# Sorting edges by destination block: four bf16 pieces per edge instead of six, and two one-hots cut in halves

## What is computed

```
xn  = layernorm(x)
deg = segment_sum(edge_weight, src) + 1
norm = dinv[src] * edge_weight * dinv[dst]            # dinv = 1/sqrt(deg)
h7[src] += (xn @ W)[dst] * norm                       # over all edges, and a self-loop each
x = x + MLP(h7) + mix(xn)                             # mix: attention without softmax, and an MLP
x = x + top-2-of-8-experts(layernorm(x))
```

## Time and profile before

| | us |
|---|---|
| median of 3 runs | 4314.45 |
| the profiled execution's own time | 4289.22 |
| its span | 4287.5 |
| setup, to the first work of the sort | 80 |
| the sort's first lot | 80 to 105 |
| the sort, from GpSimd's first scatter | 105 to 730 |
| rows stage | 730 to 879 |
| all that follows | 879 to 4287.5 |

### The profile page before, as it was taken

One profiled execution on the slowest core, in us unless ns is written; L12 is line 12 of the kernel. 1 busy time (PEld: TensorE's weight loads), 2 busy tenths in 40 slices (PEclk: granted clock), 3 DMA queues, 4 the chain that ended last, 5 costly groups with the idle time before them and its releaser, 6 DMA issues. The chain is left out here.

```text
span 4287.5 us, 76667 instructions
## 1 busy us (share of the span) xinstructions
PE 3246.9 (76%) x20541; PEld 2549.1 (59%) x20541; DVE 2761.6 (64%) x7400; ACT 1581.4 (37%) x4972; POOL 2678.2 (62%) x2429
## 2 busy tenths in 40 slices
PE   5778785757776677776557777777777589999995
PEld 4556564634444444444436665666666479999985
DVE  7999997946556556565545555555555665555577
ACT  2877773421111111111003333333333255555542
POOL 1888886256666666666666666666666246666663
PEclk8888887568888888888779888888888789999998
DMA  4322222543333334333334444444444412222367
GB/s 159 46 28 28 26 28 44 179 121 112 111 112 111 110 110 115 109 111 110 100 92 133 130 126 131 130 130 132 132 132 129 148 44 70 71 70 71 119 223 269
DMA packets 292326, 466.67 MB, mean 109 GB/s; under 512 B 96007, under 2 KB 197900, under 8 KB 292239
## 3 DMA queue, kind: packets, MB, share of 16 engines
q0 software_dynamic: 139776, 272.98, 24.5%
q1 hardware_dynamic: 140127, 183.95, 13.0%
q10 hardware_dynamic: 12338, 8.71, 0.6%
HBM read 361.91 MB, written 104.56 MB: 109 GB/s over the span
## 5 line engine op out<-in xcount | busy, mean ns | idle before, releaser
L1712 POOL DMA_INDIRECT rows<-table,idx x1664 | 1594.8, 958 | 879.7 <-issue 502.3
L2014 DVE TENSOR_TENSOR acc<-acc,ps_seg 128x256 f32 x1664 | 696.6, 419 | 927.2 <-remote 774.0
L2179 PE MATMUL ps_seg<-rows,pick 128*128 128x256 f32 x3328 | 1000.2, 429 | 342.3 <-DVE acc L2014 254.3
L2179 PEld LDWEIGHTS ps_seg<-rows,pick 128*128 128x128 f32 x3328 | 662.7, 213 | 526.6 <-issue 433.0
L860 POOL DMA_INDIRECT records<-sort_rec,sort_addr x280 | 531.8, 1899 | 181.0 <-issue 91.1
L1856 DVE TENSOR_SCALAR pick<-iota_row,loc,ewt 128x128 f32<-128x128 f32 x1680 | 531.8, 365 | 11.2 <-DVE loc L1852 4.4
L2632 POOL DMA_INDIRECT y_rows<-arena,spot x204 | 295.9, 1450 | 206.5 <-issue 59.0
L2774 PE MATMUL ps_h<-arena,up_now 128*128 128x128 f32 x3264 | 401.1, 276 | 3.7 <-DVE up_now L2702 2.3
L2774 PEld LDWEIGHTS ps_h<-arena,up_now 128*128 128x128 f32 x3264 | 382.1, 193 | 7.3 <-issue 7.1
L2758 PE MATMUL ps_y<-down_now,arena 128*128 128x256 f32 x1632 | 385.9, 379 | 0.0
L1058 PE MATMUL ps_out<-acc 128*128 128x240 bf16 x1568 | 266.3, 350 | 121.9 <-DVE acc L979 121.8
(11 more groups left out here) (403 smaller groups left out, 5090.1 us busy)
## 6 DMA issues: line engine op xcount, KB each, us to landing
rows<-table,idx POOLq DMA_INDIRECT x1664
acc<-y_rows SPq DMA_DIRECT2D x20, 896.0 KB
x_early<-in_x SPq DMA_DIRECT2D x118, 128.0 KB
xn<-in_x SPq DMA_DIRECT2D x100, 128.0 KB
xT_dram<-xT SPq DMA_DIRECT2D x98, 128.0 KB
xn<-xT_dram SPq DMA_DIRECT2D x49, 256.0 KB
skip<-in_x SPq DMA_DIRECT2D x98, 128.0 KB
x_rows<-acc SPq DMA_DIRECT2D x49, 256.0 KB
```

What stands on the lines that cost most here:

```text
L1712: pool.indirect_dma_start(out=rows[:, t, :], out_offset=None, in_=k.table, in_offset=bass.IndirectOffsetOnAxis(idx[:, h, t:t + 1], 0)).the ...
L2014: dve.tensor_tensor(here, here, sums(u), ALU.add).then_inc(added[u], 1)
L2179: last = pe.matmul(sums(t), pick[:, h, t, :], rows[:, t, :], start=True, stop=True)
```

## The change

An edge is now cut into four pieces. Word 0 of a record is no longer a sum but two bf16 values side by side: the low half-words of `dst | 1 << 14` and of a word that holds the seven low bits of the weight (one of them flipped), and the row. Word 1 is the sum of two bf16 parts of the weight with its seven low bits cleared. The rows stage puts the low bits back. With four pieces the products have 2 x 2240 elements, the matmuls of `compact` 160 columns, and the spread pieces 112 elements. The lane one-hot and the block one-hot are each made by two instructions of 14 columns, and `compact` and `count` on TensorE wait for each half. Records are written by two instructions, a copy that casts to bf16 pairs and a reduction.

```diff
-PIECES = 6
+PIECES = 4
+ROW_AT = 16
+ROUND_BITS = 7
...
 def same_block(dve, s, buf, lot, cut):          # 14 columns: cut * CUT to (cut + 1) * CUT
...
 # setup, ScalarE: four casts in place of six
+low_half = lambda words: words.bitcast(BF16).rearrange("p (n two) -> p n two", two=2)[:, :, 0]
+act.activation(s.pieces[:, 0, :], low_half(tmp_i), ACT.Copy)
+act.activation(s.pieces[:, 1, :], low_half(src), ACT.Copy)
+act.activation(s.pieces[:, 2, :], short_ew, ACT.Copy)
+act.activation(s.pieces[:, 3, :], rest, ACT.Copy)
...
 # setup, VectorE, between the histogram one-hots
-dve.tensor_scalar(tmp_i, src, P - 1, 14, ALU.bitwise_and, ALU.logical_shift_left)       # behind lots 4
-dve.tensor_scalar(block_i, dst, (P - 1) << 7, None, ALU.bitwise_and)                    # 6
-dve.tensor_scalar(tmp_i, dst, P - 1, None, ALU.bitwise_and)                             # 8
-dve.tensor_tensor(rest, ew, s.pieces[:, 3, :], ALU.subtract)                            # 15
-dve.tensor_tensor(rest2, rest, s.pieces[:, 4, :], ALU.subtract)                         # 18
+dve.tensor_scalar(tmp_i, dst, 1 << DST_BITS, None, ALU.bitwise_or)                      # 6
+dve.wait_ge(ew_in, 16)
+dve.tensor_scalar(block_i, ew_bits, (1 << ROUND_BITS) - 1, 64, ALU.bitwise_and, ALU.bitwise_xor)   # 8
+dve.tensor_scalar(dst, src, P - 1, 64 << 7, ALU.bitwise_and, ALU.bitwise_or)            # 8
+dve.scalar_tensor_tensor(out=src, in0=block_i, scalar=float(P), in1=dst, op0=ALU.mult, op1=ALU.add)  # 11
+dve.tensor_scalar(tmp_i, ew_bits, -(1 << ROUND_BITS), None, ALU.bitwise_and)            # 15
+dve.tensor_tensor(rest, short_ew, s.pieces[:, 2, :], ALU.subtract)                      # 18
...
 # sort, VectorE, routes(n): the lane one-hot
-dve.tensor_tensor(in_lane[:, h, :, :]..., pairs(s.iota_b)..., lane2[:, :, :]..., ALU.is_equal).then_inc(lane_done, 1)
+for cut in range(CUTS):
+    dve.tensor_tensor(in_lane[:, h, part, :]..., pairs(s.iota_b)..., lane2[:, part, :]..., ALU.is_equal).then_inc(lane_done, 1)
...
 # sort, VectorE, leave(n): the records
-dve.tensor_reduce(rec[:, h, :, :], OUT.rearrange("p (w j) s -> p s w j", w=2), AX.X, ALU.add).then_inc(rec_done, 1)
+dve.tensor_copy(rec[:, h, :, :].bitcast(BF16)[:, :, 0:2], OUT[:, 0:2, :].rearrange("p j s -> p s j")).then_inc(rec_done, 1)
+dve.tensor_reduce(rec[:, h, :, 1], OUT[:, 2:, :].rearrange("p j s -> p s j"), AX.X, ALU.add).then_inc(rec_done, 1)
...
 # sort, TensorE, compact(n) and count(n): a wait for each half
+if at == 0:
+    pe.wait_ge(lane_done, CUTS * n + cut + 1)
...
+if c % CUT == 0:
+    pe.wait_ge(same_done, CUTS * n + c // CUT + 1)
...
 # rows, VectorE, behind each of the four joins
+dve.wait_ge(joined, n + 1)
+dve.tensor_scalar(low_bits, words[:, :, :, 0], ROW_AT + 7, (1 << ROUND_BITS) - 1, ALU.logical_shift_right, ALU.bitwise_and)
+dve.wait_ge(low_bits_done, n + 1)
+dve.tensor_tensor(words[:, :, :, 1], words[:, :, :, 1], low_bits, ALU.bitwise_or).then_inc(whole, 1)
...
 # rows, TensorE: word 1 is turned when it is whole
-pe.wait_ge(joined, g // 4 + 1)
+pe.wait_ge(joined if w == 0 else whole, g // 4 + 1)
...
 # rows and gather: fields of word 0 are masked, and spare rows are set by an OR
-dve.tensor_scalar(high_i[:, part], k.recs[:, part, 0], DST_BITS + 5, None, ALU.logical_shift_right)
+dve.tensor_scalar(high_i[:, part], k.recs[:, part, 0], ROW_AT + 5, HIGH - 1, ALU.logical_shift_right, ALU.bitwise_and)
-dve.tensor_tensor(k.recs[:, 0:TILES, 0], k.recs[:, 0:TILES, 0], high_i, ALU.max)
+dve.tensor_tensor(k.recs[:, 0:TILES, 0], k.recs[:, 0:TILES, 0], high_i, ALU.bitwise_or)
-dve.tensor_scalar(loc_i[:, h, :], now[:, :, 0], DST_BITS, None, ALU.logical_shift_right)
+dve.tensor_scalar(loc_i[:, h, :], now[:, :, 0], ROW_AT, P - 1, ALU.logical_shift_right, ALU.bitwise_and)
```

More of the change, by code:

```diff
@@ L594, in _ @@
                 two_lots_of(11)
+                dve.wait_ge(piece_done, 3)
+                dve.scalar_tensor_tensor(out=src, in0=block_i, scalar=float(P), in1=dst, op0=ALU.mult,
+                                         op1=ALU.add).then_inc(piece_done, 1)
                 numbers()
@@ L600, in _ @@
                 two_lots_of(15)
-                dve.wait_ge(piece_cast, 4)
-                dve.tensor_tensor(rest, ew, s.pieces[:, 3, :], ALU.subtract).then_inc(piece_done, 1)
+                dve.wait_ge(piece_cast, 1)
+                dve.tensor_scalar(tmp_i, ew_bits, -(1 << ROUND_BITS), None, ALU.bitwise_and).then_inc(piece_done, 1)
                 two_lots_of(16)
@@ L605, in _ @@
                 two_lots_of(18)
-                dve.wait_ge(piece_cast, 5)
-                dve.tensor_tensor(rest2, rest, s.pieces[:, 4, :], ALU.subtract).then_inc(piece_done, 1)
+                dve.wait_ge(piece_cast, 3)
+                dve.tensor_tensor(rest, short_ew, s.pieces[:, 2, :], ALU.subtract).then_inc(piece_done, 1)
                 two_lots_of(19)
@@ L906, in body @@
                 def body(n, h, i, left, with_x=False):
[L908 to L912, removed]
+                    act.wait_ge(valued_done, CUTS * (n - 1) + VALUED_CREDIT)
+                    for cut in range(CUTS):
+                        act.activation(piece2[:, h, cut, :, :, :],
+                                       s.pieces[:, :, bass.ds(n * LOT + cut * CUT, CUT)].unsqueeze(3).to_broadcast(
+                                           [P, PIECES, CUT, 2]), ACT.Copy).then_inc(piece2_done, 1)
                     act.wait_ge(moved_done, n - 1 + TWO)
@@ L966, in routes @@
                     dve.wait_ge(lane2_done, n + 1)
[L967 to L970, removed]
+                    for cut in range(CUTS):
+                        part = slice(cut * CUT, (cut + 1) * CUT)
+                        dve.tensor_tensor(in_lane[:, h, part, :].rearrange("p c (l two) -> p c l two", two=2),
+                                          pairs(s.iota_b).unsqueeze(1).to_broadcast([P, CUT, P // 2, 2]),
+                                          lane2[:, part, :].unsqueeze(2).to_broadcast([P, CUT, P // 2, 2]),
+                                          ALU.is_equal).then_inc(lane_done, 1)
                     dve.wait_ge(slot2_done, n + 1)
@@ L976, in routes @@
                     dve.wait_ge(eq_done, n + 1)
-                    for side in range(SIDES):
-                        dve.wait_ge(piece2_done, SIDES * n + side + 1)
+                    for cut in range(CUTS):
+                        dve.wait_ge(piece2_done, CUTS * n + cut + 1)
                         dve.tensor_tensor(
[L980 to L983, removed]
+                            valued[:, h, cut, :, :, :].rearrange("p v c (s two) -> p v c s two", two=2),
+                            in_slot[:, cut * CUT:(cut + 1) * CUT, :].rearrange("p c (s two) -> p c s two", two=2).unsqueeze(
+                                1).to_broadcast([P, PIECES, CUT, SLOTS_OUT // 2, 2]),
+                            piece2[:, h, cut, :, :, :].unsqueeze(3).to_broadcast([P, PIECES, CUT, SLOTS_OUT // 2, 2]),
                             ALU.mult).then_inc(valued_done, 1)
@@ L1005, in body @@
                     if left > 1:
-                        same_block(dve, s, h, n + 2).then_inc(same_done, 1)
+                        for cut in range(CUTS):
+                            same_block(dve, s, h, n + 2, cut).then_inc(same_done, 1)
                     if left > 0:
```

86 lines of the change are left out of this document (48 added, 38 removed).

## The result

The kernel after takes 4271.82 us, the median of 5 runs (4266.98 to 4274.42), against 4314.45 for the kernel before in 5 runs (4313.09 to 4317.07). The ratio is 0.990, 95% interval 0.989 to 0.991: 43 us faster (38 to 48), where 56.1 were forecast. The direction, the range and the place held. The size of the gain in the sort was 11 us too large, and that is what the experiments are about.

The account below looks back on a forecast made before the run. VectorE was taken to bound the sort at 11.17 us a lot. Sort -59.9, setup +0.7 and rows stage +3.1 gave -56.1 us, so 4258.4 us against 4314.45; own range 4250 to 4268, 8 in 10 4248 to 4284.

Parts of the forecast that it names:

- GpSimd's catches: Sort: VectorE's one-hots and products hold scatters, which then need 1.5 us more; five still fit a lot of 10.11 us.
- the opposite: Sort, rival: scatters aren't let in between one-hot halves, four instead of five per VectorE turn; 4326 to 4395 us, chance 0.06.
- VectorE's terms: Sort, per lot: products -1.167 us, two extra operations +0.13, record pair -0.02; pitch from 11.17 to 10.11 us.
- VectorE's cut counts in full: Sort: no other engine holds the pitch up, so the whole 1.06 us a lot is saved.
- The 54 pitches: Sort: 54 lots ahead of the last measured lane one-hot, each 1.058 us shorter, -57.1 us.
- Setup: Before the sort: added integer operations on VectorE, partly inside waits for TensorE; +0.7 us, between 0 and 1.5.
- Start: Start of the sort: first counts can begin on half a block one-hot, -0.7 us.
- Tail: End of the sort: last scatter ends 30.5 us behind that lane one-hot instead of 32.6, -2.1 us.
- Rows stage: After the sort: VectorE shifts and ORs the low bits back behind four joins; +3.1 us, between +1 and +5.
- ScalarE didn't: Sort, rival: ScalarE sets the lot at 10.4 us through waits for TensorE's counts; 4275 us, chance 0.05.
- the record pair wasn't dear: Sort, rival: the record's copy and reduction cost 0.68 us together, 20 us lost; 4278 us, chance 0.03.
- GpSimd binds: Sort, rival: GpSimd misses a catch and its lot is 10.8 us; 21 us lost, about 4280 to 4293, chance 0.09.

Follow-up runs that it names:

- the pieces-alone kernel: The changed kernel with the lane and block one-hots each made in one operation of 28 columns again: 3954.65 us against 3908.88 for the kernel before, ratio 1.0115.
- the halves alone: The kernel before, with six pieces, and its lane and block one-hots each made in two operations: 3916.0 us against 3908.88 for the kernel before, ratio 1.0018.
- the lane in halves: The changed kernel with the block one-hot in one operation, the lane one-hot still in two: 3852.36 us, ratio 0.9857 to the kernel before; repeated, 3854.94 against 3910.78.

## Why the prediction was right or wrong

**The bound.** Right: VectorE set the pace before and sets it after. Without GpSimd's scatters the two sorts get shorter by 0.4% and 2% only.

**GpSimd's catches.** Right: five starts in the forecast's order, to 0.11 us in one lot and 0.22 in the next, stretched to 2.03 and 2.12 us in turn, at most 1.95 forecast. The rule "a scatter is caught once by a one-hot or product, then needs 1.5 us" also works out the pieces-alone kernel, whose lot of 11.99 us is the sum of its catches. Laid over every scatter between 130 and 640 us of the eleven traces with scatters, it gives the duration to 0.06 us for 2672 of 2677, if the catch is put 0.01 us behind the scatter's start. The prediction's 0.05 is too late: in the halves alone the scatter at 411.92 begins 0.03 us ahead of the second product and takes 1.55. That the halves hand over inside a one-hot was right. The prediction gave the opposite 0.06, and what it cost the halves at (+0.13; 0.07 each from start to start, and 0.11 net in the lot of the halves alone) was the smaller part of what they do: with four pieces and no halves the kernel is 46 us slower than before.

**VectorE's terms.** In the two kernels without scatters they can be read from start to start. The products give back 1.167, as forecast. The two extra operations cost 0.138 for 0.13. The record pair gains nothing (0.33 on the mean for 0.33) where 0.02 was forecast, and the last reduction of ranks takes 0.01 more. That adds up to 1.02 a lot of VectorE's own, where 1.058 was forecast: 54 x 0.04 = 2 us.

**The step that failed** is "VectorE's cut counts in full", with the half-sentence it rests on, that reductions from PSUM and the small operations don't hold a scatter. That looked at one direction only. In the other, a scatter can hold a small operation of VectorE, and the new arrangement set the cast of `q` on the stretch of a scatter where it does, in every lot. 54 x 0.156 = 8.4 us. It is made up of 0.14 from that cast and 0.055 on the mean from `low_i`, less the 0.04 that `low_i` cost already. The trace of before had this hint of it. There, between 135 and 640 us, `low_i` and its neighbour of the same form, `high_i`, read (count, busy us, mean ns, idle):

```profile
L958 DVE TENSOR_SCALAR sort_low_i<-sort_q_i 128x28 int32<-128x28 int32 x46 | 10.0, 217 | 0.0
...
L956 DVE TENSOR_SCALAR sort_high_i<-sort_q_i 128x28 int32<-128x28 int32 x46 | 8.0, 173 | 0.0
```

217 ns against 173. Without scatters `low_i` too takes 173. This hold is at another place than that of the cast: `low_i` begins at 583.33, and a scatter at 583.34. So the hint said that scatters can hold small operations, and not that the cast would be held.

**The sum.** The 54 pitches of the lane one-hot shrank by 46.4 us, from 602.5 to 556.1 (93.48 to 695.96 before, 92.74 to 648.87 after), where 57.1 were due; this is the one large miss. Setup +0.64 (the sort's first work at 80.82 for 80.18), +0.7 forecast. Start: the first lane one-hot came 0.7 us earlier although setup ended 0.64 later, so 1.4 for 0.7. Tail: from that last lane one-hot to the last scatter's end 32.6 us before and 30.7 after, so 1.9 for 2.1. Rows stage +3.4 for +3.1: the join, shift and OR at 694.09 to 696.42 are the three instructions that were costed. Together 45.6 us at the cast of the rows stage and 45.9 at the gather stage, for 56.1.

**The rivals.** GpSimd didn't bind (VectorE waits for no buffer), ScalarE didn't (its wait for TensorE's counts fell to 26.4 us in total, and VectorE doesn't wait ahead of its cast), and the record pair wasn't dear. Two of the prediction's figures don't stand, without weight for its sum. The price of "GpSimd binds" doesn't follow from its own lot of 10.8: less 10.11 that is 0.69 a lot, 54 x 0.69 = 37 us, and not 54 x 0.39 = 21. And the 28 products of 4.73 us ran only in part at the lower clock: the granted clock from 410.41 to 415.14 was 0.64. ScalarE's wait after the change:

```profile
ACT acc L898 <- PE ps_addr L1039: 26.4, 41, 5.0
```

## What to carry to other kernels

Where VectorE runs beside indirect DMAs of GpSimd, cost both directions: what VectorE's large operations do to a scatter, and what a scatter does to the casts and copies that land on it. A saving on one engine shifts the phase between the two, and the phase can be worth more than the saving: here much the same saving gave +46 or -56 us, depending on one extra edge. So lay the other engine's starts over the new lot before counting a cut in full, and look for small operations whose mean differs from that of neighbours of the same form.

## What the runs showed of the hardware

A small SBUF-to-SBUF cast of VectorE (28 or 56 elements a partition, 0.18 or 0.19 us long) that begins 0.52 to 0.76 us behind the start of an indirect scatter is held, and ends 1.03 to 1.08 us behind that start. All 282 such casts in the sorts of the eleven traces with scatters do so. In the kernel after the cast at 410.31 ends at 410.63, 1.03 behind 409.60; in the four pieces alone these two do, which take 0.18 and 0.19 us in the kernel after, beside a scatter that began at 402.53:

```profile
403.15 0.43 DVE L972 CAST sort_lane<-sort_lane_i 128x56 bf16<-128x56 int32 x1
403.26 0.34 DVE L974 CAST sort_slot<-sort_slot_i 128x56 bf16<-128x56 int32 x1
```

Casts that begin 0.47 us behind a scatter's start (the one at 413.14 with the lane in halves) and 1.5 behind aren't held, nor is a reduction at 0.7, nor were the casts from PSUM at 0.64 to 0.72. Casts aren't the only ones: the address operation, a `tensor_tensor` on SBUF, was held too where it began 0.65 to 0.85 us behind a start, 13 times, and ended at 1.04 to 1.08; at 0.64, in half of the lots before, it wasn't. `low_i` showed two smaller holds: up to 0.05 us where it begins within 0.02 us of a scatter's start, and 0.11 us at 1.24 behind one, in every second lot; why only there stays open. What a scatter does at these moments no run shows. The runs place it and price it.
